# A four-stage attention block on one core: where batch 1's transposed x stands in the load queue, and when VectorE copies the folded values' first half

## The reference

```
query = x @ Wq;  keyt = enc @ Wk;  valt = enc @ Wv        # enc: 73 context rows
hs     = mha(query, keyt, valt)                            # 8 heads of 20
ca_q1  = (ca @ Wq_ca)[:, indices]                          # ca: 4 tokens, 96 rows repeated to 512
ca_hs1 = mha(ca_q1, x, x)                                  # x is keys and values here
ca_hs2 = mha(ca_hs1 @ Wq, ca @ Wk_ca, ca @ Wv_ca)
out    = (hs + ca_hs2) @ Wout + b_out + x
```

## Time and profile before

| | |
|---|---|
| median of three executions | 1015.6 us (1014.93 to 1016.07) |
| the profiled execution's own time | 1019.83 us |
| its span, first to last instruction | 1018.0 us |
| mean granted TensorE clock | 0.993 |
| busy TensorE, VectorE, ScalarE, GpSimd | 974.7, 683.6, 588.9, 377.5 us |
| the adapter's share of the span | about 0 to 147 us |

### The profile page before, as it was taken

The page is one execution under the profiler, slowest core; times in us unless marked ns, Lnnn a source line. Parts: engine busy times, 40 slices in busy tenths (PEclk is TensorE's granted clock), DMA queues, the critical chain, the costliest instruction groups (busy, mean ns, idle before and its releaser), DMA issues.

```text
span 1018.0 us, 17405 instructions
## 1 busy us (share of the span) xinstructions
PE 974.7 (96%) x6346; PEld 700.8 (69%) x6346; DVE 683.6 (67%) x1164; ACT 588.9 (58%) x1326; POOL 377.5 (37%) x486
## 2 busy tenths in 40 slices
PE   7999989999999999999999999999999989999998
PEld 3566665666567666567666567666566689998887
DVE  3666737776674776674776674776636879999463
ACT  3665636666764666764666764666735455445442
POOL 3576714443332443332444332434311034444120
PEclk9999999999999999999999999999999999999999
DMA  9310230000000000000000000000001330000000
GB/s 268 102 42 2 55 96 1 1 2 1 1 2 1 1 1 2 1 1 1 1 1 1 2 1 2 1 1 1 2 1 36 104 83 1 1 2 1 2 27 26
DMA packets 19585, 22.18 MB, mean 22 GB/s; under 512 B 1366, under 2 KB 17070, under 8 KB 19502
## 3 DMA queue, kind: packets, MB, share of 16 engines
q1 hardware_dynamic: 19502, 21.09, 7.3%
HBM read 15.83 MB, written 1.31 MB: 17 GB/s over the span
## 4 chain that ended last, share of the span: by engine, by line
PE 66%; DVE 10%; ACT 4%; issue 4%; POOL 1%; DMA 0%; SPq 0%; DVEq 0%; ACTq 0%; POOLq 0%
PE banks L413 13%; PE banks L400 12%; PE banks L386 11%; PE banks L420 4%; PE banks L228 3%; ACT sa_probs L503 3%; PE banks L1626 3%; PE banks L229 2%; PE banks L231 2%; PE banks L230 2%; PE banks L1918 2%; DVE ca_top L1761 2%; PE banks L236 2%; DVE ca_probs L1766 2%; DVE sa_negmax L575 1%
## 5 line engine op out<-in xcount | busy, mean ns | idle before, releaser
L647 POOL TENSOR_SCALAR sa_probs<-sa_probs,sa_inverse 128x512 f32<-128x512 f32 x320 | 217.7, 696 | 362.6 <-DVE sa_inverse L579 362.5
L503 ACT ACTIVATE sa_probs<-banks,sa_negmax 128x512 f32<-128x512 f32 x320 | 215.9, 686 | 125.7 <-DVE sa_negmax L575 125.6
L575 DVE TENSOR_REDUCE sa_negmax<-banks 128x2 f32<-128x1024 f32 x160 | 188.7, 1218 | 10.3 <-PE banks L386 7.3
L400 PEld LDWEIGHTS banks<-ident,sa_probs 128*128 128x128 f32 x1280 | 144.4, 140 | 55.6 <-issue 27.6
L400 PE MATMUL banks<-ident,sa_probs 128*128 128x128 f32 x1280 | 172.5, 275 | 10.0 <-ACT sa_turned L514 5.6
L584 DVE COPY sa_turned<-banks 128x512 f32<-128x512 f32 x160 | 110.2, 688 | 75.3 <-PE banks L400 75.3
L413 PE MATMUL banks<-sa_turned,sa_v 128*64 128x512 f32 x640 | 155.0, 605 | 0.0
L386 PE MATMUL banks<-sa_k_parts,sa_q_parts 64*128 64x512 f32 x960 | 133.1, 408 | 1.9 <-ACT sa_probs L503 1.9
L514 ACT COPY sa_turned<-banks 128x512 f32<-128x512 f32 x160 | 94.3, 589 | 58.1 <-PE banks L400 56.3
L386 PEld LDWEIGHTS banks<-sa_k_parts,sa_q_parts 64*128 64x128 f32 x960 | 84.0, 184 | 30.4 <-issue 14.1
L413 PEld LDWEIGHTS banks<-sa_turned,sa_v 128*64 128x64 f32 x640 | 38.7, 136 | 74.2 <-issue 73.0
(11 more groups left out here) (205 smaller groups left out, 1701.9 us busy)
## 6 DMA issues: line engine op xcount, KB each, us to landing
ad_x_t<-in_x_turned SPq DMA_DIRECT2D x4, 512.0 KB, 5.0
ad_x_pad<-in_x_padded SPq DMA_DIRECT2D x4, 512.0 KB, 8.8
w_o<-in_L_xattn_wo SPq DMA_DIRECT2D x2, 800.0 KB, 9.0
x<-in_x SPq DMA_DIRECT2D x1, 1280.0 KB, 9.1
out<-x SPq DMA_DIRECT2D x4, 320.0 KB, 2.4
w_q_t<-in_L_xattn_wq_t SPq DMA_DIRECT2D x1, 1120.0 KB, 10.6
fold_values<-ca_turned SPq DMA_DIRECT2D x5, 192.5 KB
fold_values<-ca_probs SPq DMA_DIRECT2D x4, 192.5 KB
```

Source lines behind the costliest of these rows:

```text
L400: last = pe.transpose(b_turn[e][:, q * P:(q + 1) * P], probs[:, j % 2, e, q, k * P:(k + 1) * P], ident[:])
L503: act.activation(probs[:, j % 2, e, q, :], b_scores[u % 2][:, e, :], ACT.Exp, bias=negmax[:, u % RING, e:e + 1], accum_out=total[:, u % RI ...
L575: dve.tensor_reduce(negmax[:, u % RING, :], b_scores[u % 2], AX_X, ALU.max, negate=True).then_inc(s_max.sem, 1)
L647: pool.tensor_scalar(probs[:, j % 2, e, q, :], probs[:, j % 2, e, q, :], inverse[:, u % RING, e:e + 1], 1.0, ALU.mult, ALU.mult).then_inc( ...
```

## The change

In SP's list batch 1's transposed x moves from behind the first split weight to the place ahead of batch 0's padded x, and x moves from ahead of the first split weight to behind it. In VectorE's list the copy of the folded values' first half moves ahead of the query tile's sum `inverses(u)`; the second half stays behind it. No instruction is added or taken away.

```diff
             sp.dma_start(ident[:], t["ident"]).then_inc(s_ident, 16)
+            turned_x(1)
             padded_x(0)
             sp.dma_start(flat(wo[:]), t["wo_padded"]).then_inc(s_wo, 16)
             sp.dma_start(b_o[:], w("b_out").unsqueeze(0).broadcast_to([P, D])).then_inc(s_wo, 16)
             sp.dma_start(expand[:], t["expand"]).then_inc(s_wo, 16)
+            split_weights(0)
             sp.dma_start(x[:], tiles).then_inc(s_x_in, 16)
-            split_weights(0)
-            turned_x(1)
             split_weights(1)
             padded_x(1)
             split_weights(2)
...
-            def copy_folded(b):
-                if b >= 2:
+            def copy_folded(b, half):
+                if b >= 2 and half == 0:
                     dve.wait_ge(s_o.sem, s_o.at((b - 2) * QT + QT - 1, 0))
-                for half in range(2):
-                    item = ("folded", b, half)
-                    ring.wait_made(dve, item)
-                    n = min(3, CH - 3 * half)
-                    dve.tensor_copy(flat(folded[:, b % 2, 3 * half:3 * half + n, :]), ring.bank(banks, item)[:, 0:n * D]).then_inc(ring.s_dve, 1)
+                item = ("folded", b, half)
+                ring.wait_made(dve, item)
+                n = min(3, CH - 3 * half)
+                dve.tensor_copy(flat(folded[:, b % 2, 3 * half:3 * half + n, :]), ring.bank(banks, item)[:, 0:n * D]).then_inc(ring.s_dve, 1)
...
                 if 0 <= u - 1 < NU:
                     copy_end(u - 1)
+                if k == 3 and b < B:
+                    copy_folded(b, 0)
                 if 0 <= u < NU:
                     inverses(u)
                 if k == 3 and b < B:
-                    copy_folded(b)
+                    copy_folded(b, 1)
```

## The result

The changed kernel takes 1009.78 us in the median of five executions (1007.07 to 1011.95), against 1015.6 before: a ratio of 0.9943, 95% interval 0.9926 to 0.9959. The forecast was 1006.7, a gain of 8.9 us. The measured gain is 5.8 us in the first comparison and, by the ratio, 3.8 in the second. The direction was right and the size was not: part one, the loads, was forecast at 5.16 us and gives little or nothing in the median, while part two, the copy, gives what was forecast and a little more. (The copy alone gave 4.3 us in experiment 2, so that between 1.5 us and nothing is left for the loads; measured alone, in experiment 1, they gave nothing.)

A forecast was written before the change was run, and what follows sets the result against it. TensorE, busy 96% of the span, bounds the kernel, so gains come from its idle or slow-clock time. 5.16 us from the loads plus 3.75 from the copy make 8.9, taking 1015.6 to 1006.7 us; range 1004.2 to 1009.8.

The forecast's parts named there:

- part one: Slots 1 to 3: issuing batch 1's transposed x earlier removes PE's wait before the projection, gaining 5.16 us.
- part two: Slots 3, 7, 11 and 15: copying the folded values' first half before the sum saves PE 3.75 us.
- PE starts the projection at 18.09: Slot 1: with transposed x landed in time, the query projection starts at 18.09 us instead of 21.92.
- PE had nothing to do from 18.09 us: Slot 1: PE idled 3.83 us for transposed x, and the clock fall behind this gap cost another 1.63.
- the chain `max1(2)`, `exp1(2)`: Slots 2 and 3: this chain is late next, leaving about 0.7 us of PE idle before `scores1(3)` at 24.19.
- The 0.5 for slot 15: Slots 15 and 16: the second transpose needs half 1, whose copy ends 0.5 us earlier, so 0.5 is gained, not 1.2.
- The first-in-first-out queue: VectorE: sums stand behind a copy waiting for PE's fold; at most 2.4 us in all, but nothing was subtracted.
- The clock falls elsewhere: Rival, chance 0.10: a 1.7 us fall like that at the self-attention's start comes or goes; 1005.0 or 1008.4 us.
- Part one gives only part: Rival, chance 0.04: other engines' chains in slots 2 and 3 don't keep up; 3.53 instead of 5.16, 1008.3 us.
- no wait for padded x: Rival, chance 0.01: PE waits at `products1(0, 0)` for padded x; each microsecond after 25.2 costs one.
- none of `turn_probs` for POOL: Slots 4, 8, 12: POOL holding transposes would eat part two, 1010.4 us if all 3.75 go; rival's chance 0.07.

The follow-up runs named there:

- experiment 2: Kernel before with only the copy of the folded values' first half moved, loads in the old order: 1010.67 us, ratio 0.9958.
- experiment 1: Kernel before with only the loads reordered, VectorE's list unchanged: 1015.38 us in the median of 11 executions, ratio 1.0001.
- before again (9): Kernel before run once more without an edit, for a second profile: 1015.63 us.
- changed again (3): Changed kernel run once more without an edit, in a second comparison: 1010.74 us, ratio 0.9963 to before.
- experiments 4: Kernel before with `WARM = 5` in place of 3, two more dummy products at the start: 1014.4 us, ratio 0.9993.
- Experiment 7: Kernel before with one extra full-array dummy product behind PE's first real product: 1016.97 us in 12 executions, ratio 1.0009.
- experiments 5: Changed kernel with one extra full-array dummy product behind PE's first real product: 1009.59 us, ratio to before 0.9935.
- 6: Changed kernel with two extra full-array dummy products, the second ahead of `scores0(0)`: 1008.23 us, ratio to before 0.9933.
- 10: Kernel before with the loads reordered and two extra full-array dummy products in the head: 1015.24 us in 12 executions, ratio 0.9973.
- 11: Kernel before with two extra full-array dummy products in the head: 1014.56 us in 12 executions, ratio 0.9986.
- 8: Changed kernel with `WARM = 5`, two more dummy products at the very start: 1010.27 us, ratio to before 0.9945.
- experiment 12: Changed kernel with two extra full-array dummy products and `WARM = 2`, one product less at the start: 1015.0 us, ratio 0.9981.

## Why the prediction was wrong

The profiles side by side, each of one execution; times in us, "way" is the time from `scores1(1)` to `scores1(3)`, and the last column is the distance from `scores1(3)` to the self-attention's first product:

| kernel, its profile's own time | `scores1(1)` | projection of slot 1 | `scores1(3)` | way | self-attention | distance |
|---|---|---|---|---|---|---|
| before, 1019.83 | 15.16 | 21.92 | 29.35 | 14.19 | 147.13 | 117.78 |
| before again (9), 1015.63 | 19.17 | 22.22 | 28.07 | 8.90 | 145.59 | 117.52 |
| loads alone (1), 1014.67 | 18.57 | 21.33 | 27.47 | 8.90 | 145.18 | 117.71 |
| changed, 1010.50 | 18.83 | 21.59 | 27.73 | 8.90 | 141.25 | 113.52 |
| changed again (3), 1007.07 | 15.10 | 17.86 | 24.00 | 8.90 | 137.71 | 113.71 |

The self-attention's first product is this line in the timelines of PE of before again and of the changed kernel:

```profile
145.59 0.47 PE L228 MATMUL banks<-ln_y_hi,wa_hi 128*128 128x512 f32 x1 [1.90 <-issue]
...
141.25 0.47 PE L228 MATMUL banks<-ln_y_hi,wa_hi 128*128 128x512 f32 x1 [1.90 <-issue]
```

**The step that failed** is "PE starts the projection at 18.09", and before it "PE had nothing to do from 18.09 us" with the 3.83 and the 1.63 us that part one was to give. They were right for the execution that was profiled, and the experiments show that this was not the usual one. In the 67 executions of before in the comparisons of experiments 1 to 12, 45 had a mean clock of 0.995 and a median of 1015.33 us, like experiment 9, whose profile has the long head. That the others of the 45 had it too is inferred from clock and time together. In such an execution the head ends at about 22 us, when the load lands. Removing the load's delay there removes nothing: the way from `scores1(1)` to `scores1(3)` is 8.90 us before and after. With the heads of experiments 4 and 2 it was 9.10 and 9.69 with the loads in the old order, so up to 0.8 us is left for part one there. The loads alone measured a ratio of 1.0001, and loads and copy together (0.9963) no more than the copy alone (0.9958) in the same comparison. The profile gave a sign: its 1019.83 us lies 4.2 above the median of 1015.6, and the prediction named this and went on to subtract the same sum from both. The wait is the smaller part of these 4.2 us, though: the self-attention begins at 147.13 against 145.59 in experiment 9, 1.54 later, and the rest lies behind it, where the profiled execution has two more falls, at 820 to 825 and 940 to 944 us, each 3.4 us long and worth 1.7. So the 12 executions of before at 0.992 or 0.993, with a median near 1019.5, need not have had the short head and the long wait: a long head with late falls has such a mean too. They were 1 of 21, 2 of 17 and 9 of 29 in the three comparisons.

**What held of part one.** The load lands in time, nothing moved back made anything wait, and the chain `max1(2)`, `exp1(2)` is what is late next, with 0.55 us of idle forecast as 0.7. With the head of the profiled execution the forecast gain to slot 3 was 5.16 and experiment 3 shows 29.35 - 24.00 = 5.35. So the mechanism was right for an execution with a quick head, and the term was wrong for the median.

**Part two** was forecast at 3.75 us and gives 117.78 - 113.52 = 4.26 by the first pair of profiles, and 4.0 against experiment 9; the copy alone measured 4.3. Most of the surplus is in slot 3, where the way from `scores1(3)` to the projection was 7.80 us and is 34.34 - 27.73 = 6.61, 1.19 less instead of 0.86. The 0.5 for slot 15 was right in kind: half 1 is the releaser there, with 0.5 us of wait left where 1.2 was the earlier trace rows. The first-in-first-out queue, which the Trainium skill ("TensorE: Matmul & The Clock Gate", "Architectural detail") has for VectorE, cost nothing here: the trace agrees that the sum stands behind the copy, but the copy sits in what was idle time, and the sum starts 0.01 us later than it did.

**The rivals.** "The clock falls elsewhere" came closest and was priced too low. It was given 1.7 us and a place behind the adapter; the fall that counts stands in the head, lasts from 9.2 to 16 us, and moves `scores1(1)` by 18.83 - 15.10 = 3.73. That a fall can differ from one execution to the next was named, with the page of the Trainium skill, as something that one profile can't show; the runs now show it. What the prediction missed is that the wait it meant to remove was what hid this. "Part one gives only part" came true as a number and not as a mechanism: the chain over `exp1(2)` kept up, with 0.55 us of idle. The other rivals did not occur: no wait for padded x, none of `turn_probs` for POOL beyond those of before.

**What stays open.** Experiment 7 lies above before by 1.3 us in the median with an interval that includes no change; that an early arrival can cost there is shown by two profiles, the one of experiment 7 and the first of before, and by no median. What makes an execution fall into the long or the short head is not known: with the same kernel both occur. With full products in the head none of the profiles of experiments 5, 6, 7, 10 and 11 has a fall there; without them, and with `WARM = 3`, four of six have one. Falls of 3.4 us at other places differ from execution to execution too (between 104 and 113 us in experiments 2, 5, 8 and 10; at the start of the self-attention in all profiles but those of 4 and 6). At 1.7 us each they are as large as most of the differences between medians here, and whether a variant changes how often they come is open.

## What to carry to other kernels

A wait for a load is a cover for everything ahead of it: before its length is put into the sum, ask how far what it hides can vary from execution to execution, above all the granted clock, and price the gain for the usual execution. If the profiled execution's own time lies clearly outside the timed ones (here 1019.83 against 1014.93 to 1016.07), its stalls need not be those of the median: look where the excess lies, take a second profile if one can be had, and subtract from the median only what the usual execution has. A copy that holds up another engine goes into idle time ahead of a wait on the same engine for nothing.

## What the runs showed of the hardware

PE can be busy in each microsecond and still lose its clock: in the head of the changed kernel it fell at about 9.2 us, while PE worked without a gap shown on products of 4 and then of 96 rows, and stayed at 1.2 GHz until 16 us. In all five profiles with dummy products over the full array between them (and `WARM = 3`) it stayed up there, at some 0.9 us for each product (`scores1(1)` at 16.02 and 17.04 against 15.10 without), and the kernel came out no slower for them (1008.23 us against 1009.78 and 1010.74 in other comparisons; the intervals overlap, so that it is faster isn't shown). And the clock in a profile's stretches is 1.00 until the first change on record: in experiment 12 the stretches from 5 to 20 us say 1.00, while the products took twice their time.
